# A fused cross-attention and feed-forward kernel: four tile sums moved from VectorE to ScalarE and GpSimd, two tiles' statistics moved to VectorE, and the columns of four more tiles read from a second layout of x

## The reference

```python
def _L0_xattn_ref(embeds, patch_embeds, patch_lens, W_in, b_in, g_res, g_init):
    h = rmsnorm(embeds, g_res)
    h = einsum('bld,ed->ble', h, W_in) + b_in
    h_patch = rmsnorm(patch_embeds, g_init)
    return _hnet_depool(h, h_patch, patch_lens)   # first-order scan over the context rows,
                                                  # one row of it gathered and added for each row of h
def _L0_ffn_ref(x, w1, b1, w2, b2):
    h = gelu(einsum('bse,eh->bsh', x, w1) + b1)
    return einsum('bsh,he->bse', h, w2) + b2

x = x + _L0_xattn_ref(_layernorm(x), ctx_2048, mask_BxS2_if0, ...)
x = x + _L0_ffn_ref(_layernorm(x), w1, b1, w2, b2)
```

## Time and profile before

| | before |
|---|---|
| median of 3 runs | 831.66 us (831.65, 831.66, 832.69) |
| the profiled execution's own time | 834.93 us |
| its span in the profile | 833.2 us |
| PE busy | 822.3 us, 99% of the span |
| DVE, ACT, POOL busy | 315.9, 294.0, 258.0 us |
| granted clock of TensorE | 1.00 |

### The profile page before, as it was taken

The page is one execution under the profiler, slowest core; times in us unless marked ns, Lnnn a source line. Parts: engine busy times, 40 slices in busy tenths (PEclk is TensorE's granted clock), DMA queues, the critical chain, the costliest instruction groups (busy, mean ns, idle before and its releaser), DMA issues.

```text
span 833.2 us, 10703 instructions
## 1 busy us (share of the span) xinstructions
PE 822.3 (99%) x3722; PEld 675.9 (81%) x3722; DVE 315.9 (38%) x513; ACT 294.0 (35%) x542; POOL 258.0 (31%) x238
## 2 busy tenths in 40 slices
PE   7999999999999999999999999999999999999998
PEld 5877878788888888888888888888888888888886
DVE  5899852665141423233332423143113411241112
ACT  5668446422622253224422262222222222222221
POOL 2254659940633035301630062305300250011000
PEclk9999999999999999999999999999999999999999
DMA  9988994260236022602233113302300240010001
GB/s 227 281 263 282 291 301 153 89 163 22 68 102 160 0 76 88 167 7 74 72 113 80 50 58 103 50 0 101 51 1 1 79 72 0 0 50 1 1 0 51
DMA packets 39057, 78.11 MB, mean 94 GB/s; under 512 B 6369, under 2 KB 6369, under 8 KB 37265
## 3 DMA queue, kind: packets, MB, share of 16 engines
q1 hardware_dynamic: 30052, 65.95, 24.3%
q0 software_dynamic: 4608, 8.39, 6.4%
q10 hardware_dynamic: 4368, 3.42, 1.5%
HBM read 51.02 MB, written 22.84 MB: 89 GB/s over the span
## 4 chain that ended last, share of the span: by engine, by line
PE 81%; POOL 7%; DVE 4%; DMA 3%; issue 2%; SPq 1%; ACT 1%; ACTq 0%; POOLq 0%; DVEq 0%
PE acc L889 13%; PE acc L890 13%; PE acc L891 13%; PE h_bank L889 13%; PE h_bank L890 13%; PE h_bank L891 13%; DMA xa_odd<-in_x_dram 2%; POOL w_lo L545 2%; PE t_bank L948 2%; POOL x_cur L651 1%; POOL x_next L577 1%; DMA scan_table<-cl_next 1%; POOL cl L564 1%; POOL w_lo L551 1%; DVE h_lo L1070 1%
## 5 line engine op out<-in xcount | busy, mean ns | idle before, releaser
L1303 DVE TENSOR_TENSOR h_lo<-g_f,h_hi 128x512 fp32r<-128x512 f32 x128 | 101.1, 790 | 432.1 <-ACT g_f L826 432.1
L824 ACT ACTIVATE h_hi<-h_bank,b_c 128x512 fp32r<-128x512 f32 x128 | 87.9, 687 | 429.5 <-PE h_bank L891 425.9
L889 PE MATMUL h_bank<-xt_hi,w_hi 128*128 128x512 f32 x512 | 199.9, 390 | 0.6 <-POOL w_lo L545 0.6
L889 PE MATMUL acc<-w_hi,h_hi 128*128 128x512 f32 x512 | 199.8, 390 | 0.0
L891 PE MATMUL h_bank<-xt_hi,w_lo 128*128 128x512 f32 x512 | 199.3, 389 | 0.0
L890 PE MATMUL h_bank<-xt_lo,w_hi 128*128 128x512 f32 x512 | 199.2, 389 | 0.0
L891 PE MATMUL acc<-w_hi,h_lo 128*128 128x512 f32 x512 | 199.2, 389 | 0.0
L890 PE MATMUL acc<-w_lo,h_hi 128*128 128x512 f32 x512 | 199.2, 389 | 0.0
L889 PEld LDWEIGHTS h_bank<-xt_hi,w_hi 128*128 128x128 f32 x512 | 96.1, 188 | 20.7 <-issue 1.0
L891 PEld LDWEIGHTS h_bank<-xt_hi,w_lo 128*128 128x128 f32 x512 | 96.1, 188 | 20.0
L891 PEld LDWEIGHTS acc<-w_hi,h_lo 128*128 128x128 f32 x512 | 96.1, 188 | 20.0
(11 more groups left out here) (168 smaller groups left out, 701.1 us busy)
## 6 DMA issues: line engine op xcount, KB each, us to landing
out_dram<-x_cur SPq DMA_DIRECT2D x32, 256.0 KB, 2.1
x_next<-x_part SPq DMA_DIRECT2D x7, 1024.0 KB, 5.0
w_raw<-in_L_ffn_w_dram SPq DMA_DIRECT2D x6, 1024.0 KB, 9.0
scan_table<-cl SPq DMA_DIRECT2D x6, 896.0 KB
ch<-in_ctx_dram SPq DMA_DIRECT2D x20, 256.0 KB, 2.9
cl<-in_ctx_dram SPq DMA_DIRECT2D x5, 1024.0 KB
xa_odd<-in_x_dram SPq DMA_DIRECT2D x16, 256.0 KB, 7.3
x_part<-xa_odd SPq DMA_DIRECT2D x16, 256.0 KB, 3.9
```

Of the source, the lines that this page charges most:

```text
L824: act.activation(h_hi[:, m % HB, :], h_bank[m % 2][:], ACT.Gelu, bias=b1_c[:, m:m + 1])
L889: nc.tensor.matmul(dst, a_hi, b_hi, start=first, stop=False)
L1303: dve.tensor_tensor(h_lo[:, m % HB, :], g_f32[:], h_hi[:, m % HB, :].bitcast(F32), ALU.subtract).then_inc(h_split, 1)
```

## The change

**Sums of tiles 13, 15, 17 and 19** (`BY_POOL`). DVE's `tile_add` of them goes. ACT multiplies the product by the scale from PSUM into one half of `ch` (`scale_sums`, at its turn t+1, behind `tile_high`), and POOL adds that to the tile (`add_scaled`, at the head of its turn t+1). PE waits for ACT's counter before it uses the bank again, and SP waits for POOL's before it stores the tile. Counts of `acc_read` are renumbered.

**Statistics of tiles 21 and 23** leave `ON_ACT`: DVE makes them at its turns 17 and 19, where ACT made them at its turns 15 and 17.

**Tiles 16 to 19 are HOSTED too.** PE no longer turns them. Tiles 16 to 19 take the part of `w_raw` that tiles 28 to 31 had; tiles 28 to 31 use it after them, and are loaded at SP's turns 21 and 22. SP's turns 5 to 10 have two such loads each, as before, now of tiles 16 to 27.

```diff
-ON_ACT = (6, 8, 10, 18, 20, 21, 22, 23, 24, 25, 26, 27)
+ON_ACT = (6, 8, 10, 18, 20, 22, 24, 25, 26, 27)
+BY_POOL = tuple(range(13, 20, 2))
+BY_DVE = tuple(t for t in range(NT) if t not in BY_POOL)
+ND = len(BY_DVE)
-HOSTED = tuple(range(20, NT))
+HOSTED = tuple(range(16, NT))
+PLACES = 12
...
-            q = 1 + u // K
+            q = (3, 1, 2, 3)[u // K]
...
+        def wait_read(engine, t):
+            if t in BY_POOL:
+                engine.wait_ge(sums_scaled, BY_POOL.index(t) + 1)
+            else:
+                engine.wait_ge(acc_read, BY_DVE.index(t) + 1)
...
             def store_x1(t):
-                wait_apart(sp, acc_read, t + 1)
+                if t in BY_POOL:
+                    wait_apart(sp, pool_added, BY_POOL.index(t) + 1)
+                else:
+                    wait_apart(sp, acc_read, BY_DVE.index(t) + 1)
...
-                if 5 <= t < 5 + len(HOSTED) // 2:
-                    for u in (2 * (t - 5), 2 * (t - 5) + 1):
+                if 5 <= t < 5 + PLACES // 2 or t in (21, 22):
+                    for u in (2 * (t - 5), 2 * (t - 5) + 1) if t < 21 else (2 * (t - 15), 2 * (t - 15) + 1):
+                        if u >= PLACES:
+                            wait_apart(sp, x_lo, HOSTED[u - PLACES] + 1)
                         sp.dma_start(columns(HOSTED[u]), x_cols[HOSTED[u], :, :]).then_inc(cols_loaded[u], 16)
...
                 if t == 22:
+                    wait_apart(sp, pool_added, len(BY_POOL))
                     load_high_half(NA, 0)
...
+            def add_scaled(t):
+                n = BY_POOL.index(t)
+                pool.wait_ge(sums_scaled, n + 1)
+                pool.tensor_tensor(xa(t), xa(t), ch[:, n % 2, :], ALU.add).then_inc(pool_added, 1)
             for t in range(NT):
+                if t - 1 in BY_POOL:
+                    add_scaled(t - 1)
...
+            def scale_sums(t):
+                n = BY_POOL.index(t)
+                act.wait_ge(h_used, t + 1)
+                act.wait_ge(ra_ready, t + 1)
+                if n >= 2:
+                    act.wait_ge(pool_added, n - 1)
+                u = t % XR
+                act.activation(ch[:, n % 2, :], p_bank[t % 3][:], ACT.Copy, scale=ra[:, u:u + 1]).then_inc(sums_scaled, 1)
...
                 if 2 <= t < NT - 2:
                     tile_high(t + 2)
+                if t - 1 in BY_POOL:
+                    scale_sums(t - 1)
...
                 if t >= 3:
-                    pe.wait_ge(acc_read, t - 2)
+                    wait_read(pe, t - 3)
...
-                if t > 0:
+                if t > 0 and t - 1 in BY_DVE:
                     tile_add(t - 1)
```

More of the change, by code:

```diff
@@ L319, in xattn_ffn @@
         acc_read = sem("acc_read")
+        sums_scaled = sem("sums_scaled")
+        pool_added = sem("pool_added")
         w_hi_done = sem("w_hi_done")
@@ L456, in _ @@
                 if t == 29:
-                    wait_apart(sp, x_lo, HOSTED[K])
+                    wait_apart(sp, x_lo, HOSTED[2 * K])
                     load_w1(1)
@@ L462, in _ @@
             store_x1(NT - 1)
-            wait_apart(sp, x_lo, HOSTED[2 * K])
+            wait_apart(sp, x_lo, HOSTED[3 * K])
             load_w1(2)
@@ L488, in group @@
                 for i in range(TI):
-                    wait_apart(sp, acc_read, NT + TI * g + i + 1)
+                    wait_apart(sp, acc_read, ND + TI * g + i + 1)
                     sp.dma_start(out_v[g, :, i, :], x_cur[:, i, :]).then_inc(out_stored, 16)
@@ L990, in _ @@
                 project(t)
-            pe.wait_ge(acc_read, NT - 2)
+            pe.wait_ge(acc_read, ND - 2)
             pe.wait_ge(block_ready, NA)
@@ L1012, in ffn2 @@
                 if m == 0:
-                    pe.wait_ge(acc_read, NT + TI * g)
+                    pe.wait_ge(acc_read, ND + TI * g)
                 if m < 12:
```

## The result

| | before | after |
|---|---|---|
| median | 831.66 us (831.57 to 833.3, 5 runs) | 836.0 us (835.22 to 836.88, 5 runs) |
| ratio, 95% interval | | 1.0049 (1.0037 to 1.0061): 4.1 us slower (3.1 to 5.1) |
| the profiled execution's own time, and its span | 834.93 us, 833.2 us | 836.88 us, 834.9 us |

The kernel is slower by 4.1 us, where 0.8 us was forecast. The two profiled executions differ by only 1.95 us, because the one of before stood 3.3 us above its median and the one of after 0.9 us. That already warns against reading the change as the difference of two single traces.

A forecast was written before the change was run, and what follows sets the result against it. PE, busy 99%, bounds the kernel through when it leaves the first stage; DVE's terms (+0.2, +0.89, -0.66, +0.36) give +0.8 us at block 1's store, shifting everything behind: 831.66 becomes 832.5 us, range 830.5 to 834.0.

The forecast's parts named there:

- I take +0.36 for each of the two: DVE turns 17 and 18: each subtraction beside POOL's adds takes 0.36 us longer, bounds 0 and +0.99.
- The two low parts: DVE's subtractions for tiles 19 and 20, expected to run beside POOL's adds at +0.36 us each.
- the sum: DVE's delays and savings added up: +0.2 us at tile 19's low part, +0.8 at block 1's last `add_carry`.
- 1.4 us to spare: DVE turn 14: time from the end of `one_hots_p` to 69.9, said to cover what POOL's first add costs DVE.
- its upper bound: Skill's rule for DVE's two subtractions: each could wait up to a whole add, making the sum 1 to 2 us worse.
- row of 1.04: Profile row of a two-SBUF DVE subtraction, 1.04 us against 0.68, read as the one time beside POOL's adds.
- POOL's floor: POOL's own program before the gather, ready at 91.6 against the table's landing at 91.7: a second gate.
- paths were level: End of first stage: PE's own tiles, and DVE-SP-DMA-POOL, which sets the last turn by 0.65 us; a gain needs both.
- The table lands late: Rival: block 1's table lands 2 us later on top of 0.8, or both subtractions wait 0.99 each; 834.2 us, chance 0.17.
- the delayed table: Block 0's store, held by `store_x1(15)` behind POOL, enters saturated DMA; block 1 lands 2 us later on top of 0.8.
- Both signs cancel: Rival: POOL's adds cost DVE nothing, or the table flies 1.5 us faster; 830.9 to 831.9 us, chance 0.21.
- faster: Rival: DVE stays ahead, PE keeps its 1.9 us from transposes, table lands by 89.0; 829.8 us, chance 0.09.

The follow-up runs named there:

- e5: Changed kernel with VectorE's `count_rows` moved from its turn 17 to turn 15, before POOL's adds start; 834.89 us, ratio 1.0041.
- e7: Kernel before with two more 128x512 additions, read by nobody, on POOL at its turn 17; 834.06 us, ratio 1.0022.
- f3: e9 with tile 19's sum back on VectorE and POOL's adds held back behind the low parts they would meet; 834.07 us, ratio 1.0027.
- e1: Kernel before, unchanged, run again for a second profile; 832.0 us, ratio 0.9999.
- e4: Changed kernel with tiles 16 to 19 turned by PE again, with the loads and waits of before; 835.44 us, ratio 1.0039.
- e6: Changed kernel with POOL's four `add_bias` moved behind VectorE's `count_rows`; 834.54 us, ratio 1.0030.
- e8: Changed kernel with ACT's `scale_sums(13)` one turn earlier, so POOL's first add comes before `one_hots_p`; 834.83 us, ratio 1.0031.
- g1: Changed kernel with SP's two stores to the table issued in front of the other work of their turns; 836.46 us, ratio 1.0054.
- g3: f3 with SP's two stores to the table issued in front of the other work of their turns; 832.36 us, ratio 1.0005.
- f1: Kernel before with only the columns of tiles 16 to 19 hosted, sums and statistics as before; 832.42 us, ratio 1.0010.
- e3: Changed kernel with the statistics of tiles 21 and 23 back on ACT; 834.64 us, ratio 1.0030.
- e9: Changed kernel with the edits of e3, e5 and e8 joined; 833.62 us, ratio 1.0022.

## Why the prediction was wrong

- **The step that failed** is the price of VectorE beside GpSimd: "I take +0.36 for each of the two". It was put on too few instructions, more than it was too small. The two low parts that it meant cost 0.43 and 0.25. But two more places met POOL's adds: tile 17's low part (+0.73), and `count_rows` (+1.86), which the sum never named, since its three instructions are 0.18 us each in the trace of before. e5 and e7 show the count's share: away with it in the changed kernel 1.1 us (roughly, by its interval), alone in the kernel before 2.0. An instruction that has to wait for the engine beside it costs what it waits for, not its own length.
- **Why two such adds, and not none.** Before, POOL's adds ended before the count (74.44 + 4.69 = 79.13, the count at 79.4). The prediction wrote down that POOL would now add from 75.0 to 82.8 without a break, and looked beneath that stretch only for subtractions.
- **Tile 17.** POOL's first add was meant to fall beside `one_hots_p`, with 1.4 us to spare after it. It waited for `one_hots_p` itself (3.01 us instead of 1.3) and so pushed `add_bias(0)` onto tile 17's low part, 67.99 to 69.29 against 68.42.
- **The rule of the Trainium skill** (SBUF — State Buffer, "Who interferes with whom") was weighed in the prediction, for these two subtractions alone, and the nearest row of 1.04 us was taken instead. The traces bear the rule out in every instruction looked at. At those two places its upper bound, a whole add each, was not reached (0.43 and 0.25); the loss came from the places not listed. It should have been run over every two-operand instruction in POOL's stretch, in both directions. `add_carry`, with one operand in PSUM, took 2.47 us for four in f3, beside POOL's adds at 77.06 and 78.31, and 2.47 in e1, without them.
- **The row of 1.04 was misread.** The prediction calls it the one time that POOL's adds ran beside such a subtraction. It is at 102.59, and beside it POOL ran its subtractions for the weights' low half:

```profile
102.59 1.04 DVE L1070 TENSOR_TENSOR h_lo<-w_raw,h_hi 128x512 fp32r<-128x512 f32 x1
101.78 6.01 POOL L545 TENSOR_TENSOR w_lo<-w_raw,w_hi 128x512 fp32r<-128x512 f32 x4
```

  The first of POOL's four ran from 101.78 to 103.07, and DVE's subtraction began 0.5 us before its end. The 0.36 is what was left of that one meeting, and no price for another.
- **POOL's floor** was rightly seen as a second gate, just in time at 91.6 against 91.7. It lacked the 0.98 us from the indices to the gather (the same in after, e4, e6, e8, g1 and g3), and hung on DVE's statistics of tile 23, which came at 87.49 instead of 86.7. So it became the gate, and the row of the gather, in after as in g1, shows that the table no longer was. This puts the last turn 0.67 us behind PE's own tiles.
- **The base.** The shift was worked out on a trace whose paths were level, and carried over to the median. In e1 the gather comes at 88.52, its values reach PE without a wait, and the level does not exist. In absolute times the forecast looks good: the store of block 1 at 84.7 (85.42), the gather at 92.6 (93.45), the last turn at 115.3 (115.94), tile 21 near 86.0 (86.66). But the trace of after began 1.6 us earlier at tile 16 (64.40 against 65.99), and so 3.1 us of loss on DVE looked like 1.3 to 1.7 against the first trace (tile 21 +1.28, the last turn +1.44, the store +1.50, the gather +1.66). Two errors nearly hid each other there, and not in the median.
- **Right:** the shift that counts is DVE's at tile 21 and in `add_carry`; `tile_add(13)` was worth nothing (DVE idle 1.09 and 0.86 us for ACT); `scale_sums` takes 0.57 from start to start (0.47); block 0's store at 78.85 (79); `tile_stats(21)` 0.89; the columns of tiles 28 to 31, issued at 91.55 and 93.44, are hidden; the transposes' 1.9 us go in waiting (f1).
- **The rivals.** "The table lands late", 834.2, named the doubled contention as one of its ways and was still 1.8 us short. Its other way, the delayed table, shows only once DVE is relieved: SP issues block 1's store 0.1 us after DVE's end in the kernel after, but 0.8 us after it in e3, 2.2 in e5 and e9, and 3.3 in f3. "Both signs cancel" and "faster" didn't occur.
- **The sum, mended:** 3.1 for DVE up to tile 21, less 0.3 that PE had to spare there (e1: ready at 82.19 + 0.68 = 82.87, start 83.15), and 0.7 for the last turn behind POOL's gate, of which e1 has nothing: 3.5, against 4.1 measured, interval 3.1 to 5.1, and 3.6 in the trace of g1. How the 1.4 us of the statistics (e3) divide between DVE's instructions and POOL's gate, which both moved (gather 92.58 instead of 93.45), stays open; POOL's add of tile 19 fell on tile 21's low part there and made it 1.43 us long.

## What to carry to other kernels

When work moves to GpSimd, lay its new busy stretch over VectorE's program and list every instruction there with two SBUF inputs, the shortest too: each can wait for most of a GpSimd instruction (one of 0.18 us took up to 1.22 here, beside adds of 1.3), and in a chain of small ones it can happen again (to two of three here). An engine that is idle for half of the time is not free, if its work blocks the one that is full. And compare a profiled execution's own time with the median before its paths are called level: here it stood 3 us above, and a second trace showed another picture.

## What the runs showed of the hardware

- A 128x8 addition on VectorE, 0.18 us alone, took 1.05 to 1.22 us beside GpSimd's adds of 128x512 (1.3 us each), in the kernel after and in e7.
- GpSimd is blocked as well: 3.01 us for an add of 1.3, beside one VectorE instruction of 1.88 us.
- In the traces of after, e7 and e8 the granted clock is 0.83 between 10 and 20 us, in the other fourteen it is 1.00. In the trace of after the products there start 0.43 us apart, at the level of 1.2 GHz, from 12.7 to about 16.4 us, and 0.23 apart after that, at 2.4 GHz. PE had waited 1.98 us for DVE just before (1.94 in e7, 1.98 in e8), but in e4, e5 and e9 it had waited 1.98 us too and the clock stayed at 1.00, so the wait alone does not decide it. Tile 16's low part comes 0.8 us later for it (64.40 against 63.64 in g1). Of the 108 executions of the kernel before beside the experiments, the 15 with a mean granted clock of 0.998 have a median of 832.8 us, the 84 with 1.00 one of 831.9; of the five of the changed kernel only the profiled one has 0.998, so its median does not hang on this.
- The issue of one DMA on SP's queue takes 0.3 to 0.4 us at some places and 1.7 to 2.3 us at others around 80 us; a store that has only to be issued can be 3 us late for it (f3).
